# Gram matrices in four 32-column tiles, and a longer pipeline around them

## The reference, cut to what matters

```python
# block 0, per sample, both directions; rgb = x.T, geo = y.T, scale = 16 ** -0.5
attn = softmax(einsum('bhni,bhnj->bhij', q, k) * scale)   # q, k, v: 1x1 maps of rgb or geo
res_p2r = xca(rgb@wq_rgb.T, geo@wk_point.T, geo@wv_point.T) @ proj_p2r.T
res_r2p = xca(geo@wq_point.T, rgb@wk_rgb.T, rgb@wv_rgb.T) @ proj_r2p.T
x1 = (rgb + res_p2r).T + (geo + res_r2p).T
# block 1: queries and keys from y, values from x1, all with biases
attn = softmax(einsum('bhdl,bhel->bhde', Wq@y+bq, Wk@y+bk) / sqrt(128))
o = Wo @ (attn @ (Wv@x1+bv)) + bo + x1
out = (o - mean(o)) * rsqrt(var(o) + 1e-5) * gn_w + gn_b  # mean, var over the whole sample
```

## Time and profile before

| | us |
|---|---|
| median of 3 runs | 351.15 (349.2 to 351.64) |
| the profiled execution | 351.63 |
| its span, first to last instruction | 349.7 |
| PE busy (share of the span) | 335.8 (96%) |
| ACT | 251.5 (72%) |
| DVE | 230.7 (66%) |
| POOL | 188.9 (54%) |

### The profile page before, as it was taken

How to read it: one execution, slowest core, us unless ns; L and a number is a source line. 1 busy time by engine, 2 the same in 40 slices (tenths; PEclk the granted TensorE clock), 3 DMA queues, 4 the chain that set the end, 5 groups by cost and what they waited for, 6 DMA issues and landing times.

```text
span 349.7 us, 8291 instructions
## 1 busy us (share of the span) xinstructions
PE 335.8 (96%) x2678; PEld 281.5 (80%) x2678; DVE 230.7 (66%) x649; ACT 251.5 (72%) x410; POOL 188.9 (54%) x277
## 2 busy tenths in 40 slices
PE   6999999999999999999999999999999999999980
PEld 3788888797888889788888979888887988887760
DVE  2365694848668494866759485675948576692864
ACT  2546787778778787778878777887878787786332
POOL 0673892754819184572919467390937639092010
PEclk9899999999999999999999999999999999999995
...
GB/s 232 382 119 243 178 201 186 205 214 236 179 275 180 274 148 219 201 189 255 180 275 177 247 174 192 254 146 272 180 221 185 199 242 49 120 0 122 0 43 200
DMA packets 29643, 66.39 MB, mean 190 GB/s; under 512 B 2368, under 2 KB 16960, under 8 KB 29632
## 3 DMA queue, kind: packets, MB, share of 16 engines
...
...
HBM read 49.47 MB, written 16.78 MB: 189 GB/s over the span
## 4 chain that ended last, share of the span: by engine, by line
PE 92%; DVE 3%; issue 2%; DMA 1%; ACT 1%; SPq 0%; POOLq 0%; POOL 0%
PE gacc L359 33%; PE oacc L379 9%; PE oacc L384 8%; PE oacc L380 8%; PE tpx L316 7%; PE mid L469 4%; PE mid L403 4%; PE mid L446 4%; PE mid L455 2%; PE mid L406 2%; PE mid L456 2%; DMA raw<-in_ctx 1%; PE mid L458 1%; PE mid L457 1%; PE mid L416 1%
## 5 line engine op out<-in xcount | busy, mean ns | idle before, releaser
L1013 POOL TENSOR_TENSOR xy_lo<-raw,xy_hi 128x256 fp32r<-128x256 f32 x256 | 177.8, 733 | 128.3 <-ACT xy_hi L631 128.3
L359 PE MATMUL gacc<-t 128*128 128x257 f32 x512 | 126.2, 389 | 0.8 <-ACT t L563 0.8
L359 PEld LDWEIGHTS gacc<-t 128*128 128x128 f32 x512 | 93.4, 192 | 14.8 <-issue 2.6
L631 ACT ACTIVATE xy_hi<-raw 128x1024 fp32r<-128x1024 f32 x64 | 67.1, 1051 | 0.0
L783 DVE STREAM_TRANSPOSE t<-y_blocks 128x512 f32<-128x512 f32 x56 | 64.5, 1152 | 0.0
L379 PE MATMUL oacc<-xy_hi,pq_hi 128*128 128x512 f32 x124 | 51.9, 419 | 0.4 <-ACT pq_hi L610 0.2
L380 PE MATMUL oacc<-xy_lo,pq_hi 128*128 128x512 f32 x124 | 48.9, 395 | 0.0
L563 ACT ACTIVATE t<-tpx 128x512 f32<-128x512 f32 x64 | 38.0, 597 | 9.3 <-PE tpx L329 8.4
L638 ACT ACTIVATE res<-oacc 128x512 f32<-128x512 f32 x60 | 35.7, 595 | 11.6 <-PE oacc L384 9.9
L794 DVE BATCH_NORM_STATS2 hstat<-res 128x6 f32<-128x512 f32 x60 | 39.4, 676 | 6.2 <-ACT res L638 6.2
L384 PE MATMUL oacc<-xy_hi,pq_lo 128*128 128x512 f32 x124 | 39.0, 395 | 0.0
...
## 6 DMA issues: line engine op xcount, KB each, us to landing
raw<-in_x SPq DMA_DIRECT2D x31, 512.0 KB, 7.8
raw<-in_ctx SPq DMA_DIRECT2D x31, 512.0 KB, 9.4
...
out<-res ACTq DMA_DIRECT2D x28, 512.0 KB, 6.4
out<-res SPq DMA_DIRECT2D x4, 512.0 KB, 2.6
...
```

The lines of the kernel that those rows point to most:

```text
L359: mm = pe.matmul(gacc[:, 0:2 * C + 1], t[slot][:, c, C:2 * C], t[slot][:, c, :], start=(c == 0), stop=(c == CH - 1))
L631: act.activation(xy_hi[slot][:, s, :], raw[slot][:, s, :], ACT.Copy).then_inc(split_hi, 1)
L1013: piece = pool.tensor_tensor(xy_lo[slot][:, s, cols], raw[slot][:, s, cols], xy_hi[slot][:, s, cols].bitcast(f32), ALU.subtract)
```

## The change

- **Gram in four tiles.** `t` is now [y | 1 | x], 257 columns. A chunk is no longer one product of 128 output partitions, but six products of 32 (L368 to L373 in the new file), each with 32 columns of y as weights. Each output row block of 32 gets 225 of the 257 columns: the x block and the sums, and three of its four 32-column blocks of y y^T. The fourth is the transpose of a block that another row block has. `gram_mirror` fills it in, on DVE, with four 32x32 block transposes for both samples of the pair, and only `u3_products` (the part of `u_products` that reads y y^T) waits for it.
- **A bank for each sample.** The second sample's Gram goes into bank `stat`, beside the statistics' few columns, so that the second Gram needn't wait until the first is copied out. PE waits for `var_ready` before it.
- **Order.** On PE the scores, both Grams and `z_products` stand in a row, with the four transposes of the second sample ahead of them. `pq_products` moves from the end of a step to the start of the next one, as do the last `split_high` and `split_low`, the statistics, their `group_moments`, `deviation`, `normalise` and the stores. `steps` has two more steps outside the loop, which now makes 6 turns.
- **Loads.** The four `y_blocks` DMAs of a sample each fill 32 partitions with 4 pieces of 1 KB, instead of 128 partitions with one piece. `abv` (L907) is computed ahead of the four `attn` products instead of behind them.

The diff, cut (ACT's and the remaining steps are reordered in the same way; where they matter, the prediction says it):

```diff
 W32 = 32
+XC = C + 1
+GW = XC + C
 TB = 4
 PIECES = 4
...
-        t = [sb(f"t{n}", [C, CH, 2 * C + 1]) for n in range(TB)]
-        gram = sb("gram", [C, 2, 2 * C + 1])
+        t = [sb(f"t{n}", [C, CH, GW]) for n in range(TB)]
+        gram = sb("gram", [C, 2, GW])
...
-        mean_s, abv_s = stat[:, 16:18], stat[:, 32:34]
+        mean_s, abv_s = stat[:, 16:18], mid0[:, 12 * W32:12 * W32 + 2]
+        gacc_b = [gacc[:, 0:GW], stat[:, H64:H64 + GW]]
...
         def steps(eng, step):
-            step(0, 0, True, False, False)
-            step(0, 1, True, True, False)
-            with eng.Fori(1, PAIRS // 2) as i:
-                step(i, 0, True, True, True)
-                step(i, 1, True, True, True)
-            step(PAIRS // 2, 0, False, True, True)
-            step(PAIRS // 2, 1, False, False, True)
-
-
+            step(0, 0, True, False, False, False)
+            step(0, 1, True, True, False, False)
+            step(1, 0, True, True, True, False)
+            step(1, 1, True, True, True, True)
+            with eng.Fori(2, PAIRS // 2) as i:
+                step(i, 0, True, True, True, True)
+                step(i, 1, True, True, True, True)
+            step(PAIRS // 2, 0, False, True, True, True)
+            step(PAIRS // 2, 1, False, False, True, True)
+
+        def before(h, u):
+
+            return (h - 1, 0) if u == 1 else (h - 2, 1)
...
-                blocks = y[4 * h + n].rearrange("(i c) (a m) -> i a c m", c=W32, a=QUADS)
-                for i in range(QUADS):
-                    sp.dma_start(y_blocks[n][:, i, :], blocks[i]).then_inc(blocks_in[n], 16)
+                blocks = y[4 * h + n].rearrange("(i c) (a m) -> a c i m", c=W32, a=QUADS)
+                for a in range(QUADS):
+                    sp.dma_start(y_blocks[n][W32 * a:W32 * (a + 1), :, :], blocks[a]).then_inc(blocks_in[n], 16)
...
-                if begin == 0 and end == CH:
-                    pe.wait_ge(xt_ready, 2 * n + 2)
-                    pe.wait_ge(yt_ready, 2 * n + 2)
-                elif begin % HC == 0:
+                tb, acc = t[slot], gacc_b[b]
+                if begin % HC == 0:
                     pe.wait_ge(xt_ready, 2 * n + begin // HC + 1)
                     pe.wait_ge(yt_ready, 2 * n + begin // HC + 1)
-                if begin == 0 and not (isinstance(n, int) and n < 1):
-                    pe.wait_ge(gram_ready, n)
+                if begin == 0 and not (isinstance(n, int) and n < 2):
+                    pe.wait_ge(gram_ready, n - 1)
                 for c in range(begin, end):
-                    mm = pe.matmul(gacc[:, 0:2 * C + 1], t[slot][:, c, C:2 * C], t[slot][:, c, :],
-                                   start=(c == 0), stop=(c == CH - 1))
+                    first, final = c == 0, c == CH - 1
+                    wa, wb, wc, wd = (tb[:, c, W32 * j:W32 * (j + 1)] for j in range(QUADS))
+                    pe.matmul(acc[0:W32, C:GW], wa, tb[:, c, C:GW], start=first, stop=False)
+                    pe.matmul(acc[3 * W32:C, 3 * W32:GW], wd, tb[:, c, 3 * W32:GW], start=first, stop=False)
+                    pe.matmul(acc[W32:H64, W32:GW], wb, tb[:, c, W32:GW], start=first, stop=final)
+                    pe.matmul(acc[H64:3 * W32, W32:GW], wc, tb[:, c, W32:GW], start=first, stop=final)
+                    pe.matmul(acc[0:W32, 0:3 * W32], wa, tb[:, c, 0:3 * W32], start=False, stop=final)
+                    mm = pe.matmul(acc[3 * W32:C, 0:H64], wd, tb[:, c, 0:H64], start=False, stop=final)
...
-            def u_products(p):
+            def u12_products(p):
...
-                    pe.wait_ge(pqlo_ready, p)
                     pe.wait_ge(c_ready, p)
                 for a in range(2):
                     dst = mid0[:, a * 2 * C:(a + 1) * 2 * C]
-                    mm = pe.matmul(dst, gram[:, a, 0:C], wt[:, 0:2, :], start=True, stop=True)
+                    mm = pe.matmul(dst, gram[:, a, XC:GW], wt[:, 0:2, :], start=True, stop=True)
                 mm.then_inc(u12_done, 1)
+
+            def u3_products(p):
+
+                pe.wait_ge(gram_full, p + 1)
+                if not (isinstance(p, int) and p < 1):
+                    pe.wait_ge(pqlo_ready, p)
                 for a in range(2):
-                    mm = pe.matmul(mid1[:, a * C:(a + 1) * C], gram[:, a, C:2 * C], w("kT"), start=True, stop=True)
+                    mm = pe.matmul(mid1[:, a * C:(a + 1) * C], gram[:, a, 0:C], w("kT"), start=True, stop=True)
...
                 elif front:
                     x_transpose(h, u, 0, 0)
                     x_transpose(h, u, 0, 1)
-                    u_products(p - 1)
+                    pq_products(p - 2)
+                    u12_products(p - 1)
+                    if post:
+                        group_moments(p - 3)
                     out_half(h - 1, u, 0, 0)
+                    u3_products(p - 1)
+                    x_transpose(h, u, 1, 0)
+                    x_transpose(h, u, 1, 1)
                     out_half(h - 1, u, 0, 1)
                     scores(p - 1)
+                    gram_chunks(h, u, 0, 0, 4)
+                    gram_chunks(h, u, 0, 4, 8)
+                    if post:
+                        pe.wait_ge(var_ready, p - 2)
+                    gram_chunks(h, u, 1, 0, 4)
+                    gram_chunks(h, u, 1, 4, 7)
+                    z_operands(p - 1)
+                    gram_chunks(h, u, 1, 7, 8)
+                    z_products(p - 1)
                     out_half(h - 1, u, 1, 0)
                     out_half(h - 1, u, 1, 1)
-                    x_transpose(h, u, 1, 0)
-                    gram_chunks(h, u, 0, 0, 3)
-                    z_operands(p - 1)
-                    gram_chunks(h, u, 0, 3, 4)
-                    z_products(p - 1)
-                    gram_chunks(h, u, 0, 4, 8)
-                    x_transpose(h, u, 1, 1)
-                    group_moments(p - 2)
                     m_products(p - 1, False)
-                    gram_chunks(h, u, 1, 0, 4)
-                    pq_products(p - 1)
-                    gram_chunks(h, u, 1, 4, 8)
...
+            def gram_mirror(p):
+
+                dve.wait_ge(gram_ready, 2 * p + 2)
+                for i, j in ((0, 3), (1, 0), (2, 0), (3, 2)):
+                    rows, cols = slice(W32 * i, W32 * (i + 1)), slice(W32 * j, W32 * (j + 1))
+                    last = dve.transpose(gram[rows, :, cols], gram[cols, :, rows])
+                last.then_inc(gram_full, 1)
...
                 elif front:
+                    if post:
+                        half_stats(*before(h, u), 1, 0)
+                        half_stats(*before(h, u), 1, 1)
+                        half_moments(p - 3)
+                        partition_moments(p - 3, 1 - u)
+                    pq_low(p - 2, u)
+                    if post:
+                        variance(p - 3, 1 - u)
...
+                if front and middle and post:
+                    deviation(p - 3)
+                if middle and back:
+                    split_low(h - 1 + u, 1 - u, 1, 1)
                 if front:
                     split_low(h, u, 0, 0)
                     split_low(h, u, 0, 1)
                     split_low(h, u, 1, 0)
-                if back and (front or middle):
+                    if not middle:
...
```

181 lines of the change are left out of this document (102 added, 79 removed).

## The result

The changed kernel takes 352.22 us (median of 18 runs, 351.08 to 354.21), the kernel before 349.97 (18 runs beside it). The ratio is 1.007, 95% interval 1.0051 to 1.0089: no gain, but a small loss of 0.7%; the interval leaves out no change at all. The forecast was 342.0 us, range 336.5 to 351. It took 9.2 us off a median of three runs, 351.15; against the 18 runs beside it the change adds 2.3 us. The profiled execution of the changed kernel has a span of 350.4 us; the forecast's sum gives 349.7 - 9.2 = 340.5, so 9.9 us have to be found. These are two single executions, and the one before (351.63 us) is at the upper end of its 18, the changed one (352.21) in the middle of its own.

A forecast was written before the change was run, and what follows sets the result against it. PE's own work was taken to bound the loop. Chunks -11.8, crossings -2.8, moments' wait +3.9, drain +1.0 and fill +0.5 sum to -9.2 us, from 351.15 to 342.0 us, range 336.5 to 351.

The forecast's parts named there:

- chunks and crossings: PE's Grams: a tiled chunk takes 0.39 us, gaining 11.8 us in all; fewer changes between array layouts gain 2.8 us.
- wait for the moments: Loop: PE waits for DVE's work ahead of `group_moments`, 0.3 us a step (bounds 0 and 0.6), +3.9 us in 13 steps.
- end of the fill: Fill: sample 1's transposes, now ahead of the first chunks, wait for its y load, +0.5 us; `pq_products` (0.89) leave.
- drain: After the loop: waits for `pq_products`, the moments and the scores' operand cost +1.0 us (0 to 2).
- A: Gram tiles: sets move together, narrow tiles idling until the widest ends; 0.55 us a chunk, 383 us; chance 0.07.
- B: Gram on PE: instruction supply too slow; at 20 ns each 0.48 us a chunk, 365 us; chance 0.07.
- D: Gram tiles: no overlap as assumed, strict program order; 0.78 us a chunk, 440 us; chance 0.02.
- rule of strict order: PE: the skill's rule that matmuls start and end in program order; set aside because the trace showed 0.12 us against 0.26.
- DVE has 6.2 us of slack a step: Loop: DVE is busy 13.98 us of a 20.21 us step, so it was taken to have room.
- rival C: Loop: DVE or ACT later than added up; a wait of 1.0 us a step leaves no gain, 347 to 352 us; chance 0.12.
- slow clock: Fill: PE's half clock may last 3.4 us more after new gaps, 0 to +1.7 us; taken as 0.

The follow-up runs named there:

- e5: Changed kernel with the products of a Gram chunk in another program order, both of one tile's products together: 354.48 us, ratio 1.0106.
- e1: Changed kernel with PE taking `group_moments` behind the first out half instead of ahead of it in the loop's steps: 352.79 us, ratio 1.0070.
- e4: Changed kernel without its tiles: order, second bank, mirror and new loads stay, each Gram chunk is one full-array product: 361.20 us, ratio 1.0305.
- e9: Changed kernel with full-array Gram chunks in the two steps of the fill alone, tiles elsewhere: 351.12 us, ratio 1.0051.
- e12: Changed kernel: moments and variance later, drain's first `deviation` earlier, one x transposition earlier, full-array Gram chunks in all four steps ahead of the loop; 345.07 us, ratio 0.9856.
- e7: Changed kernel with GpSimd taking `deviation` ahead of the last `split_low` in the drain's first step: 350.82 us, ratio 1.0028.

## Why the prediction was wrong

Step by step, in profiled spans (forecast 340.5, measured 350.4):

| term | forecast | measured | miss |
|---|---|---|---|
| chunks and crossings, a step | -0.93 | -0.96 | none |
| wait for the moments, 13 steps | +3.9 | +8.3 | +4.4 |
| the loop's first pass (a gap of 1.3 in it) | 0 | +1.7 | +1.7 |
| end of the fill | 34.3 | 36.1 | +1.8 |
| drain | 32.4 | 35.3 | +2.9 |
| the rest of the loop | | | -0.9 |

(Fill forecast: 36.34 - 0.89 + 0.5, less 32 chunks at 0.045 and a crossing of 0.19.)

- **Chunks and crossings held**, with the mechanism: free-running tiles, 0.385 us a chunk (0.39 forecast). A, B as a rate and D are refuted by the trace and by e5. The rule of strict order (the Trainium skill, TensorE: Matmul & The Clock Gate, Part 3) was rightly set aside: each tile's next record starts by its own last one alone, at 0.12, 0.16 and 0.21 us.
- **The step that failed** is the price of the moments' wait, "Sum ... a wait of 0.56. But DVE's records that need nothing of each other overlap ... I take 0.3". The series came out: `mom` stood 3.2 us after the step's start. Independent records did overlap (the two L855 start 0.12 us apart, not 0.19), but the next one, which needs both, started late (L862 0.12 us behind the second's end), so that little was won. The wait was 0.54 and 0.30 in turn, and the 0.27 of a weight load behind that wait had no term at all. Over the 13 steps the waits are 5.1 us and the loads 3.2: of the miss of 4.4 the load is the larger part. The measured +8.3 are the passes L415 and L404 over 13 steps less 1.01 each (0.87 + 0.14); a steady step has 0.55 or 0.78.
- **And removing that wait wouldn't have given the forecast**: e1 shows a second path of the same length through VectorE's L873, the softmax and `attn`. "DVE has 6.2 us of slack a step" was a sum of busy time; VectorE's order had none to give. This is rival C, which had 0.12. That its price, 347 to 352 us, nearly came true (352.22) is in part luck: its wait of 1.0 a step was 0.7, and fill, first pass and drain brought the rest.
- **The fill** was forecast from loads and clock. The slow clock did last 3.7 us longer (to 15.3 us), the term that was taken at 0 with 1.7 as its bound; but with full clock and tiled code the loop still starts at 35.8 to 37.4, and without the gap (e4, e9) at 34.3 and 33.6. Rival B named the supply of instructions, and its sign, issue time in a Gram, came; but it looked for it in a rate and in six later turns of the loop; it came in first passes, through the fill and the first turn, where the earlier trace rows doesn't reach (it begins at 80 us, and shows a loop half as long). That the gap is the arrival of instructions is inferred from five things: no release, only in kernels with the new order and tiles, only in a first pass, gone where the code is short (e9, e12), and a packet that ends 1.2 to 1.7 us ahead of PE's next record each time. What happens in those 1.2 to 1.7 us no row shows, nor what holds the packet back. The Trainium skill (Runtime: NRT & Kernel Launch, instruction fetch mechanics) says that the sequencer streams code in blocks of 16 KiB, 256 instructions, and that crossing into the next is mostly hidden. The packets here agree with the size (0.26 MB in 16). With the hiding they agree for the most part: only one of the 16 stands at a gap of over 1 us in the changed kernel's trace, and one to three do in the other tiled kernels of the new order but e12; but those cost 1.1 to 3.8 us each, where a chunk is 24 records and weight loads in 0.385 us. The later turns of the loop don't test it, since no packet comes in them.
- **The drain** had a term for the moved products and the moments (+1.0 forecast, with 0.89 moved in). Missed was POOL: `deviation` behind the last `split_low`, 1.3 us by e7. The rest, 1.6 us, wasn't tried. The traces say where it lies: from `z_products` to the end the two drains are alike (22.2 us, 22.6 before), but these start 13.1 us into the drain, where they started at 8.0. The first output product alone comes 2.85 us later (4.20 instead of 1.35), where the forecast had 1.9 for all of it.

The repaired order with tiles (e12) is 1.4% faster than the kernel before, 345.07 us: about half of the forecast's 2.6% was there, behind waits that the same change brought.
